# Cross-attention with layer norm: four output buffers and a last stage written out in an order of its own

## The reference

```python
Q = (query @ w_q.T).reshape(B, S, 16, 32).transpose(0, 2, 1, 3)
K = (key @ w_k.T).reshape(B, -1, 16, 32).transpose(0, 2, 1, 3)
V = (value @ w_v.T).reshape(B, -1, 16, 32).transpose(0, 2, 1, 3)
attn = softmax(einsum('bhqd,bhkd->bhqk', Q, K) / sqrt(32))
ctx = einsum('bhqk,bhkd->bhqd', attn, V).transpose(0, 2, 1, 3).reshape(B, S, 512)
x = ctx @ w_o.T + b_o + query
mu, var = mean(x), mean(square(x - mu))          # over the last axis
return (x - mu) * rsqrt(var + 1e-5) * ln_gamma + ln_beta
```

## Time and profile before

| | |
|---|---|
| time, median of 3 runs | 612.33 us (609.22 to 612.86) |
| profiled execution | 616.87 us, span 615.1 us, mean granted TensorE clock 0.977 |
| busy, share of the span | TensorE 95%, GpSimd 77%, VectorE 77%, ScalarE 73% |
| load of one x tile (256 KB), issue to landing, median | 2.9 us |
| store of one y tile (256 KB), issue to landing, median | 2.2 us |

### The profile page before, as it was taken

One profiled execution on the slowest core, in us unless ns is written; L12 is line 12 of the kernel. 1 busy time (PEld: TensorE's weight loads), 2 busy tenths in 40 slices (PEclk: granted clock), 3 DMA queues, 4 the chain that ended last, 5 costly groups with the idle time before them and its releaser, 6 DMA issues.

```text
span 615.1 us, 12235 instructions
## 1 busy us (share of the span) xinstructions
PE 582.4 (95%) x4330; PEld 462.0 (75%) x4330; DVE 472.7 (77%) x874; ACT 450.3 (73%) x799; POOL 476.6 (77%) x333
## 2 busy tenths in 40 slices
PE   8888889998999999999999999998999999999875
PEld 7655558887877888788868788886888877888553
DVE  7857348876888888888868888886888877888657
ACT  7657467867877788888777888885888777877831
POOL 4627347886988888988878888897789888878840
PEclk9989889998999999999989999998999999999988
DMA  8342213332343333433334233333334423122323
GB/s 308 126 91 58 57 42 96 95 91 92 114 116 87 114 103 104 121 115 91 102 97 120 85 109 113 102 115 88 100 104 118 114 84 93 55 71 74 108 85 120
DMA packets 79757, 62.74 MB, mean 102 GB/s; under 512 B 52272, under 2 KB 52272, under 8 KB 79696
## 3 DMA queue, kind: packets, MB, share of 16 engines
q1 hardware_dynamic: 79696, 61.96, 33.9%
HBM read 39.39 MB, written 16.78 MB: 91 GB/s over the span
## 4 chain that ended last, share of the span: by engine, by line
PE 81%; DVE 6%; ACT 4%; DMA 4%; issue 3%; SPq 1%; POOL 1%; ACTq 0%; DVEq 0%
PE ps_q L425 23%; PE ps_o L431 23%; PE ps_c L473 13%; PE ps_s L368 6%; DMA out<-y 4%; PE ps_o L393 3%; PE ps_o L307 3%; PE ps_s L307 3%; PE ps_s L379 3%; PE ps_q L307 2%; SPq L287 1%; ACT inverse L582 1%; DVE q_lo L634 1%; DVE turned L721 1%; DVE half_max L727 1%
## 5 line engine op out<-in xcount | busy, mean ns | idle before, releaser
L817 POOL TENSOR_TENSOR p_lo<-probs,p_hi 128x1024 fp32r<-128x1024 f32 x59 | 142.2, 2410 | 67.3 <-ACT p_hi L515 67.3
L425 PE MATMUL ps_q<-x_hi,wq_lo 64*128 64x512 f32 x448 | 179.1, 400 | 6.2 <-DVE q_lo L634 6.2
L431 PE MATMUL ps_o<-wo_hi,c_lo 64*128 64x512 f32 x448 | 179.1, 400 | 0.0
L431 PE MATMUL ps_o<-wo_lo,c_hi 64*128 64x512 f32 x448 | 178.2, 398 | 0.0
L425 PE MATMUL ps_q<-x_lo,wq_hi 64*128 64x512 f32 x448 | 177.4, 396 | 0.0
L425 PE MATMUL ps_q<-x_hi,wq_hi 64*128 64x512 f32 x448 | 176.9, 395 | 0.0
L431 PE MATMUL ps_o<-wo_hi,c_hi 64*128 64x512 f32 x448 | 176.8, 395 | 0.0
L425 PEld LDWEIGHTS ps_q<-x_hi,wq_lo 64*128 64x128 f32 x448 | 83.5, 186 | 17.8 <-DVE q_lo L634 10.5
L721 DVE STREAM_TRANSPOSE turned<-ps_s 128x1024 f32<-128x1024 f32 x64 | 80.0, 1251 | 14.1 <-PE ps_s L368 9.8
L431 PEld LDWEIGHTS ps_o<-wo_lo,c_hi 64*128 64x128 f32 x448 | 84.0, 188 | 8.4
L425 PEld LDWEIGHTS ps_q<-x_hi,wq_hi 64*128 64x128 f32 x448 | 83.8, 187 | 8.6
(11 more groups left out here) (123 smaller groups left out, 1436.2 us busy)
## 6 DMA issues: line engine op xcount, KB each, us to landing
xT_raw<-in_xT SPq DMA_DIRECT2D x64, 256.0 KB, 3.0
x_raw<-in_x SPq DMA_DIRECT2D x64, 256.0 KB, 2.9
out<-y SPq DMA_DIRECT2D x64, 256.0 KB, 2.2
max_rows<-max_turned SPq DMA_DIRECT2D x128, 16.0 KB
ctx_raw<-in_ctxT SPq DMA_DIRECT2D x4, 256.0 KB, 5.0
wk_raw<-in_wkT SPq DMA_DIRECT2D x4, 256.0 KB, 5.3
wq_raw<-in_wqT SPq DMA_DIRECT2D x4, 256.0 KB, 6.0
wv_raw<-in_wvT SPq DMA_DIRECT2D x4, 256.0 KB, 7.3
```

What stands on the lines that cost most here:

```text
L425: return nc.tensor.matmul(ps_q[:, 0, :], w[l][half, k, dims], x_[r][half, qc % 2, k, :], start=(half is lower and k == 0 and step == 0), s ...
L431: return nc.tensor.matmul(ps_o[:, 0, :], cx[l][half, k, tile], wo[r][half, k, :], start=False, stop=(half is lower and k == KT - 1 and ste ...
L817: nc.gpsimd.tensor_tensor(p_lo[:, :, :], probs_of(n)[:, :, :], p_hi[:, :, :].bitcast(fp32), ALU.subtract).then_inc(p_lo_done, 1)
```

## The change

1. `y` has four buffers in place of two (i % 4), with four semaphores for the stores. ScalarE writes y of tile i once the store of tile i - 4 has landed, in place of that of i - 2. x_raw, z and the statistics keep two.
2. VectorE alone finishes tiles 58, 59, 62 and 63 (BY_DVE) in place of the last six; 60 and 61 go by ScalarE and GpSimd as the others.
3. The loops of TensorE, ScalarE and VectorE end at t = 62, and what is left stands written out. The output tiles 57, 59 and 63 take bank ps_q, 60 and 61 the two banks of ps_s that slot 62 leaves, the others ps_o. Of tiles 60 to 63 the first three k (of 12 matmuls nine) are summed ahead: those of 60 and 61 before combine_values(63), those of 62 and 63 behind it; the last k of all four comes at the end.
4. The loops of GpSimd and of the SyncE queue keep their order; only their semaphore counts and buffer numbers change.

```diff
-    LAST = 6
+    BY_DVE = (58, 59, 62, 63)
...
-        y = sb("y", [P, 2, DM], fp32)
+        y = sb("y", [P, 4, DM], fp32)
...
+            return {57: ps_q, 59: ps_q, 60: ps_s, 61: ps_s, 63: ps_q}.get(i, ps_o)[:, 1 if i == 61 else 0, :]
+        def by_dve(i):
+            return sum(j <= i for j in BY_DVE)
+        def by_act(i):
+            return max(i + 1, 0) - by_dve(i)
...
 # SyncE queue
-                    if i < TILES - LAST:
-                        sp.wait_ge(y_done, i + 1)
+                    if i in BY_DVE:
+                        sp.wait_ge(last_y_done, by_dve(i))
                     else:
-                        sp.wait_ge(last_y_done, i - (TILES - LAST) + 1)
-                    sp.dma_start(out[P * i:P * (i + 1), :], y[:, i % 2, :]).then_inc(y_stored[i % 2], 16)
+                        sp.wait_ge(y_done, by_act(i))
+                    sp.dma_start(out[P * i:P * (i + 1), :], y[:, i % 4, :]).then_inc(y_stored[i % 4], 16)
...
 # TensorE, start_output
+                if i == 57:
+                    pe.wait_ge(q_lo_done, SLOTS)
+                elif i in (60, 61):
+                    pe.wait_ge(exp_done, SLOTS - 1)
                 else:
-                    pe.wait_ge(q_lo_done, SLOTS)
+                    wait(pe, z_done, {58: 57, 59: 58, 62: 59, 63: 60}.get(i, i))
...
 # TensorE, after the loop
+            score(SLOTS - 1)
+            project_output(56, range(KT))
+            subtract_max(SLOTS - 2)
+            start_output(57)
+            project_output(57, range(KT))
+            combine_values(SLOTS - 3, False)
+            combine_values(SLOTS - 3, True)
+            subtract_max(SLOTS - 1)
+            start_output(58)
+            project_output(58, range(KT))
+            start_output(59)
+            project_output(59, range(KT))
+            combine_values(SLOTS - 2, False)
+            combine_values(SLOTS - 2, True)
+            for i in (60, 61):
+                start_output(i)
+                project_output(i, range(KT - 1))
+            combine_values(SLOTS - 1, False)
+            combine_values(SLOTS - 1, True)
+            for i in (62, 63):
+                start_output(i)
+                project_output(i, range(KT - 1))
+            for i in (60, 61, 62, 63):
+                project_output(i, (KT - 1,))
...
 # ScalarE; the functions hold what the loop held
+            def normalise(i):
+                s = i % 2
+                act.wait_ge(shift_done, by_act(i))
+                wait(act, y_stored[i % 4], 16 * (i // 4))
+                nc.scalar.activation(y[:, i % 4, :], z[:, s, :], ACT.Identity, bias=shift[:, s:s + 1],
+                                     scale=rstd[:, s:s + 1]).then_inc(normed_done, 1)
+            def exponentiate(n):
+                act.wait_ge(shifted_done, n + 1)
...
+                wait(act, p_lo_done, n)
...
 # ScalarE, after the loop
+            negate_max(SLOTS - 2)
+            invert_sums(SLOTS - 4)
+            exponentials_to_hi(SLOTS - 3)
+            invert_deviation(55)
+            exponentiate(SLOTS - 2)
+            negate_max(SLOTS - 1)
+            normalise(55)
+            context_to_hi(SLOTS - 4)
+            exponentials_to_hi(SLOTS - 2)
+            invert_sums(SLOTS - 3)
+            exponentiate(SLOTS - 1)
+            invert_deviation(56)
+            normalise(56)
+            context_to_hi(SLOTS - 3)
+            invert_deviation(57)
+            normalise(57)
+            exponentials_to_hi(SLOTS - 1)
+            invert_sums(SLOTS - 2)
+            invert_deviation(58)
+            invert_deviation(59)
+            context_to_hi(SLOTS - 2)
+            invert_sums(SLOTS - 1)
+            context_to_hi(SLOTS - 1)
+            for i in (60, 61):
+                invert_deviation(i)
+                normalise(i)
+            for i in (62, 63):
+                invert_deviation(i)
...
 # VectorE, after the loop
+            turn_max(SLOTS - 2)
+            turn_scores(SLOTS - 1)
+            shift_mean(55)
+            half_maxima(SLOTS - 1)
+            fold_up(SLOTS - 1)
+            fold_halves(SLOTS - 1)
+            add_residual(56)
+            turn_max(SLOTS - 1)
+            divide(SLOTS - 4)
+            statistics(56)
+            shift_mean(56)
+            add_residual(57)
+            statistics(57)
+            divide(SLOTS - 3)
+            shift_mean(57)
+            for i in (58, 59):
+                add_residual(i)
+                statistics(i)
+            divide(SLOTS - 2)
+            finish(58)
+            finish(59)
+            divide(SLOTS - 1)
+            for i in (60, 61):
+                add_residual(i)
+                statistics(i)
+                shift_mean(i)
+            for i in (62, 63):
+                add_residual(i)
+                statistics(i)
+            finish(62)
+            finish(63)
...
 # GpSimd
-                if 0 <= i < TILES - LAST:
-                    s = i % 2
+                if 0 <= i < TILES and i not in BY_DVE:
+                    s = i % 4
```

More of the change, by code:

```diff
@@ L477, in _ @@
             project_queries(0)
-            for t in range(SLOTS + OUT_LAG):
+            for t in range(SLOTS - 1):
                 n, i = t + 1, t - OUT_LAG
-                if n < SLOTS and i >= 0:
+                if i >= 0:
                     project_both(n, i, False)
@@ L569, in _ @@
                 split_x(u)
-            for t in range(SLOTS + OUT_LAG + 2):
-                steady = OUT_LAG <= t < SLOTS
-                if 0 <= t - 1 < SLOTS and not steady:
-                    negate_max(t - 1)
[L575 to L598, removed]
-                i = t - OUT_LAG - 1
-                s = i % 2
[L601 to L608, removed]
@@ new lines, in invert_sums @@
+            def invert_sums(n, between=None):
+                act.wait_ge(c_product, n + 1)
+                if n == 0:
+                    act.wait_ge(bias_filled, 16)
+                wait(act, c_raw_done, n)
+                nc.scalar.activation(inverse[0:64, :], ps_c[64:128, 0, :], ACT.Ln)
+                nc.scalar.activation(inverse[64:128, :], ps_c[0:64, 1, :], ACT.Ln).then_inc(log_sum_done, 1)
+                if between is not None:
+                    negate_max(between)
+                act.wait_ge(log_sum_done, n + 1)
+                nc.scalar.activation(inverse[:, :], inverse[:, :], ACT.Exp, scale=-1.0).then_inc(inverse_done, 1)
@@ new lines, in _ @@
+            for t in range(SLOTS - 1):
+                steady = t >= OUT_LAG
+                if t >= 1 and not steady:
+                    negate_max(t - 1)
+                if t >= 3:
+                    invert_sums(t - 3, t - 1 if steady else None)
+                if t >= 2:
+                    exponentials_to_hi(t - 2)
+                if t >= 3:
+                    context_to_hi(t - 3)
+                i = t - OUT_LAG - 1
+                if i >= 0:
+                    invert_deviation(i)
@@ L696, in fold_halves @@
                                         axis=AX.X, op=ALU.max).then_inc(row_max_done, 1)
[L698 to L715, removed]
-                i = t - OUT_LAG
[L717 to L728, removed]
-                    if not both:
-                        fold_up(n)
-                        fold_halves(n)
@@ new lines, in turn_max @@
+            def turn_max(n):
+                dve.wait_ge(max_hi_done, n + 1)
+                nc.vector.tensor_reduce(max_hl[64:128, 0, :].bitcast(fp32),
+                                        max_hl[0:64, :, :].bitcast(fp32).rearrange("p h b -> p b h"),
+                                        axis=AX.X, op=ALU.add).then_inc(max_lo_done, 1)
+                dve.wait_ge(max_lo_done, n + 1)
+                wait(dve, max_rows_filled, 32 * n)
+                nc.vector.transpose(max_turned[:, :], max_hl[:, 0, :].bitcast(fp32)).then_inc(max_turned_done, 1)
@@ L732, in _ @@
+            for t in range(SLOTS - 1):
+                i = t - OUT_LAG
+                if t >= 1:
+                    turn_max(t - 1)
+                if t >= 3:
+                    divide(t - 3)
+                turn_scores(t)
+                if i >= 1:
+                    shift_mean(i - 1)
+                half_maxima(t)
+                if i < 0:
+                    fold_up(t)
+                    fold_halves(t)
                 if t in VALUES_AT:
                     values_to_lo(VALUES_AT.index(t))
-                i = t - OUT_LAG - 1
```

171 lines of the change are left out of this document (91 added, 80 removed).

## The result

| | before | changed |
|---|---|---|
| median, first chip | 611.83 us (4 runs) | 618.76 us (617.96 to 620.44, 4 runs) |
| ratio, 95% interval | | 1.0123 [1.0083, 1.0164] |
| profiled execution | 616.87 us, span 615.1 | 619.56 us, span 617.7 |
| run again on another chip | 613.45 us (13 runs) | 617.42 us (10 runs), ratio 1.007 [1.0029, 1.0111] |

The change makes the kernel slower by 4 to 7 us, where I had forecast 611.5.

The account below looks back on a forecast made before the run. TensorE was taken to bound the steady loop, with 13.8 us lost to store waits, and a serial pipeline the tail. 616.87 - 13.8 + 10.6 = 613.7 us profiled; middle with 609.2: 611.5 us, 8 in 10 within 604.5 to 618.

Parts of the forecast that it names:

- Part 1: Steady stage, 90 to 565 us: four y buffers remove ScalarE's wait for stores, -13.8 us on the profiled execution.
- rival 2: Steady loop: another transfer takes the store's place, so the gain fails and the time is 622.9 us; 11%.
- Part 2's chain: Tail's new order: p_lo(62), exp(63), shift_mean(56), z(57), tile 59, combine(62), c_lo(62), tile 60, combine(63); +7.5 us before clock effects.
- both idle stretches: TensorE in the tail: idle 3.8 us before tile 59 and 4.4 us at tile 60's third k.
- the new wait: Tail: z(57), behind shift_mean(56), invert_deviation(56) and exp(63), holds up tile 59 and combine(62); TensorE idles 3.8 us.
- Rivals 1 and 3: Tail: 1, the order pays, 594.7 us, 12%; 3, the clock stays up, +7.5, 608.4 us, counted within the forecast's 77%.
- Sum: Whole kernel: 616.87 (profiled) - 13.8 + 10.6 = 613.7 us, then taken to 611.5 us for the timed runs.
- I take the middle: Timed runs: 611.5 us, between 613.7 (one event fewer) and 609.2 (constant cost of profiling).
- +10.6 us for the tail: Tail: +7.5 us from the new order, plus 3.1 us from the lower clock behind two idle stretches.
- The second stretch at the lower clock: Tail, rest of tiles 60 and 61 after TensorE's 4.4 us idleness: lower clock adds 1.54 us.
- VectorE's ending: End of tail: VectorE's work for tiles 60 to 63 behind tile 60's product takes 11.5 us in all.
- The sign was forecast as open: Whole kernel: 68% between 606.2 and 618.5 us; faster 12% and 6%, slower 11% and 3%.

Follow-up runs that it names:

- the early sums: Before with four y buffers and moved banks, plus three quarters of tiles 60 to 63 summed first, last quarters at the end: 608.18 us, ratio 0.9936.
- the moved banks: Before with four y buffers, tile 59 moved to ps_q, 60 to ps_o, 61 and 62 to ps_s, 63 to ps_q: 601.5 us, again 600.99 us.

## Why the prediction was wrong

**What held.** The mechanism of both parts. Part 1, "-13.8 on the profiled execution": 13.76 by the trace of the four buffers alone, and no other transfer took the store's place (rival 2 falls). Part 2's chain: every link named is in the chain of waits, both idle stretches have the forecast length to 0.3 us, the lower clock follows both, and mending the link called "the new wait" gave back 4.7 us. Rivals 1 and 3 fall: the order doesn't pay, and the clock doesn't stay up.

**What failed is the step "Sum"**, and two terms of it, with a third that it put at nothing. In the profiled executions I had 613.7 and 619.56 was measured; in the medians 611.5 and 618.76.

1. "I take the middle": the gap of 4.5 us between before's profiled execution and its median could be one store event fewer or a cost of profiling, and I took half of each. No cost of profiling shows here: the profiled executions of the changed kernel and of the twelve runs behind it lie within 2.3 us of their medians, on both sides. The first reading was right and the sum was 613.7. That is 2.2 us. It also bears on what part 1 is worth: before's timed runs lose 9.7 us by the two buffers, where its profiled execution lost 13.8 in the slots alone.
2. "+10.6 us for the tail": 11.8 against before. The second stretch at the lower clock cost 2.3 us (589.62 to 595.35, 5.73 us where 3.42 are the full-speed sum) and not 1.54: 0.8 more. The other 0.4 are steps of 0.1 us along the chain, such as combine(62) and combine(63) at 2.0 each for 1.9. VectorE's ending took the forecast 11.5 us (603.77 to 615.23), though its first finishing step took 0.35 more than alone (below). Beside the four buffers alone part 2 costs still more, 13 to 14 us, since their tail is 1.35 us shorter than before's; I had given part 1 nothing in the tail.
3. Not in the sum at all: 2.7 us before the first steady slot, and 1.8 us from slots of 8.333 in place of 8.30. The runs show both to vary with one program. Most of the 2.7 us is the clock. Timeline of TensorE in the start, before and then the changed kernel, and the windows view of 59 to 66 us of both in the same order:

```profile
59.52 0.50 PE L307 MATMUL ps_o<-wv_hi,ctx_lo 128*128 128x512 f32 x1 [2.88 <-DVE values_lo L634]
```

```profile
59.63 0.80 PE L312 MATMUL ps_o<-wv_hi,ctx_lo 128*128 128x512 f32 x1 [2.88 <-DVE values_lo L705]
```

```profile
59.00:66.00 7.00, 6.42 (x34) 4.44 (x35) 1.49 (x4) 1.97 (x5) 2.58 (x3) 1.00 0.28 58
```

```profile
59.00:66.00 7.00, 6.37 (x18) 4.42 (x18) 1.60 (x4) 0.67 (x2) 2.65 (x3) 0.55 0.24 56
```

The same wait was followed by the lower clock in the one and not in the other. Behind its next wait TensorE resumes at 71.48 in before and at 74.16 in the changed kernel.

611.5 + 2.2 + 1.2 + 2.7 + 1.8 = 619.4, beside 619.56. On the second chip the changed kernel took 617.4, and there part 1 brought 9.7 us and part 2 cost 13.7, where the forecast of 611.5 amounts to 11.4 and 10.6. The sign was forecast as open: it is that of the difference of two terms of some 10 us each, and 10% of each would have been enough to turn it.

## What to carry to other kernels

Work moved ahead pays only if someone waited for it: summing three quarters of four tiles early took the last tiles' layer norms out of the shadow of TensorE and cost 6.5 us by itself. When an order is written out by hand, walk each engine's queue for a short step that others wait for and that stands behind a long wait; moving one such line gave 4.7 us. And when a change has a good and a bad part, run them apart: the four buffers alone are 9.7 us faster than before, with the banks of four of the last tiles moved 12.5, and the whole change is slower.

## What the hardware showed that I had not expected

VectorE and GpSimd slow each other down. Timeline of VectorE in the changed kernel, and GpSimd's multiplication by gamma in the same stretch:

```profile
588.46 1.66 DVE L818 SCALAR_TENSOR_TENSOR y<-y,rstd,beta_row 128x512 f32<-128x512 f32 x1
590.04 1.76 DVE L813 SCALAR_TENSOR_TENSOR y<-z,mean_var,gamma_row 128x512 f32<-128x512 f32 x1
...
611.77 1.09 DVE L813 SCALAR_TENSOR_TENSOR y<-z,mean_var,gamma_row 128x512 f32<-128x512 f32 x1
612.97 0.75 DVE L818 SCALAR_TENSOR_TENSOR y<-y,rstd,beta_row 128x512 f32<-128x512 f32 x1
```

```profile
589.53 1.73 POOL L938 TENSOR_TENSOR y<-y,gamma_row 128x512 f32<-128x512 f32 x1
```

The finishing instruction reads two tensors from SBUF. Alone it takes 0.75 us; while GpSimd combines two tensors it takes 1.58 to 1.76, and of the three GpSimd instructions beside it two take 1.60 and 1.73 us in place of 1.3, while the first (c_lo, at 588.31) keeps 1.26. VectorE's z, one operand of which lies in PSUM, isn't slowed at all. All 56 of the steady stage (count, then shortest, median and longest in ns), in which GpSimd is busy for 414 of 475 us:

```profile
L799 DVE TENSOR_TENSOR z<-ps_o,x_raw x56: 692/692/692, 97.8 to 556.2; 128x512 f32<-128x512 f32 x56
```

The Trainium skill ("VectorE: DVE Perf Modes", Two Vector instructions with no wait between them) has the second of two SBUF tensors read through an interface that is shared with GpSimd; the rows fit that, and no run here isolates it.

The lower clock isn't reserved for long idle stretches, and the same wait isn't always followed by it. TensorE waits 1.13 or 1.14 us for p_lo inside combine(63) in before and in every kernel with before's tail. The lower clock followed in both traces of the four buffers alone (at 573.9, window above) and in that of the early sums (at 574.0), and didn't in before (at 587.0) and in both traces of the moved banks.
